# Two-tile exponentials, a row-sum column in V, and PSUM copies moved from ScalarE to VectorE in a two-layer transformer kernel

## What is computed

```python
# layer 0
x = x + attn0(layernorm(x))      # 16 heads of 128, causal, ALiBi bias
x = x + ffn0(layernorm(x))       # silu(x@gate * gs) * (x@up * us) @ down * ds, weights rounded to fp8, width 6144
# layer 1
x = x + attn1(layernorm(x))      # per token, over 32 groups of 64 channels:
                                 # qkv per group; scores[d,c,e] = q[c,d]*k[e,d]/8; softmax over e; times v; @ Wout
x = x + moe(layernorm(x))        # 8 experts of width 1408, all computed; the top one is taken, with its weight

# attn0, per head
scores = q @ k.T / sqrt(128) + slope * (kpos - qpos), -inf for kpos > qpos
out    = softmax(scores) @ v     # then all heads @ wo + bo
```

## Time and profile before

| | us |
|---|---|
| median of 2 runs | 21964.12 (21844.47 and 22083.77) |
| the profiled execution's own time | 21777.46 |
| its span on the slowest core | 21775.9 (cores: 21561.0 to 21775.9) |
| mean granted TensorE clock of the cores | 0.667 to 0.682 |
| PE busy, PEld busy | 10597.1, 4188.3 |
| DVE busy | 7421.1 |
| ACT busy | 6238.7 |
| POOL busy | 1330.9 |

### The profile page before, as it was taken

How to read it: one execution, slowest core, us unless ns; L and a number is a source line. 1 busy time by engine, 2 the same in 40 slices (tenths; PEclk the granted TensorE clock), 3 DMA queues, 4 the chain that set the end, 5 groups by cost and what they waited for, 6 DMA issues and landing times.

```text
span 21775.9 us, 138456 instructions; the slowest of 8 cores (21561.0 to 21775.9 us)
## 1 busy us (share of the span) xinstructions
PE 10597.1 (49%) x42512; PEld 4188.3 (19%) x42512; DVE 7421.1 (34%) x9984; ACT 6238.7 (29%) x5808; POOL 1330.9 (6%) x1053
## 2 busy tenths in 40 slices
PE   5855555573221432115312331002886886877876
PEld 2311112221000110002100110001332332332332
DVE  1011112100688308880387607883111111111111
ACT  3466664210222102221122202222222222222222
POOL 0000000120000000001000000000001000000000
PEclk9955556786555665557655665555786776777887
DMA  3400002794221542116412450001334344343444
GB/s 66 65 9 12 9 9 34 113 47 35 25 14 13 31 41 15 12 11 41 28 12 17 23 36 10 4 4 44 56 51 48 37 42 44 33 44 42 41 46 44
DMA packets 2403671, 711.62 MB, mean 33 GB/s; under 512 B 1986923, under 2 KB 2374268, under 8 KB 2392724
## 3 DMA queue, kind: packets, MB, share of 16 engines
q0 software_dynamic: 2203008, 484.28, 29.2%
q1 hardware_dynamic: 199958, 218.48, 3.2%
HBM read 1144.49 MB, written 209.72 MB: 62 GB/s over the span
## 4 chain that ended last, share of the span: by engine, by line
PE 36%; DVE 28%; DMA 15%; ACT 11%; issue 6%; DVEq 2%; ACTq 1%; SPq 0%; POOL 0%; POOLq 0%
DVE ctxa L953 8%; PE ps_gM L1409 6%; PE ps_uM L1415 6%; DMA out<-ostrip 6%; PE ps_dM L1486 5%; DVE zz L932 5%; DVE sct L910 5%; DMA d<-dw 5%; PE ps_sh L1172 4%; PE ps_p L326 3%; ACT L610 3%; DVE sct L948 3%; DMA u<-uw 2%; PE ps_gB L1099 2%; ACT L1496 2%
## 5 line engine op out<-in xcount | busy, mean ns | idle before, releaser
L1486 PE MATMUL ps_dM<-fuseM,dwb 128*128 128x512 bf16 x5632 | 2131.5, 555 | 31.9 <-DVEq L1440 22.7
L1099 PE MATMUL ps_gB<-xn2T,g 128*128 128x512 bf16 x3072 | 964.6, 485 | 2135.9 <-DVEq L1132 1861.7
L953 DVE TENSOR_REDUCE ctxa<-sct 128x64 bf16<-128x2048 bf16 x512 | 1831.0, 3576 | 39.5 <-issue 2.1
L920 ACT ACT_TABLE_LOAD x512 | 656.9, 1283 | 3966.7 <-DVEq L912 3966.4
L214 PE MATMUL ps_tpF<-identb,ctxa 128*128 128x128 bf16 x256 | 37.4, 301 | 3317.1 <-DVEq L957 3269.9
L1409 PE MATMUL ps_gM<-xn4T,gwb 128*128 128x512 bf16 x5632 | 1456.3, 419 | 165.6 <-DMA uwb<-muw 165.6
L1172 PE MATMUL ps_sh<-fuse,d 128*128 128x512 bf16 x3072 | 833.8, 442 | 1332.4 <-DMA d<-dw 1332.4
L1529 DVE TENSOR_SCALAR ostrip<-ps_otM,cmb 128x128 f32<-128x128 bf16 x1792 | 506.1, 344 | 2737.4 <-PE ps_otM L1506 1468.9
L1415 PE MATMUL ps_uM<-xn4T,uwb 128*128 128x512 bf16 x5632 | 1438.5, 415 | 0.0
L1496 ACT ACT_TABLE_LOAD x512 | 656.9, 1283 | 2717.9 <-PE ps_dM L1486 2717.9
L910 DVE TENSOR_TENSOR sct<-qkv 128x2048 f32<-128x2048 bf16 x512 | 1173.8, 2293 | 166.2 <-DVEq L957 137.9
(11 more groups left out here) (161 smaller groups left out, 13001.8 us busy)
## 6 DMA issues: line engine op xcount, KB each, us to landing
out<-ostrip POOLq DMA_DIRECT2D x128, 1024.0 KB, 11.1
g<-gw POOLq DMA_DIRECT2D x192, 256.0 KB, 6.9
u<-uw POOLq DMA_DIRECT2D x192, 256.0 KB, 8.7
d<-dw POOLq DMA_DIRECT2D x64, 768.0 KB, 15.1
gwb<-mgw POOLq DMA_DIRECT2D x88, 512.0 KB, 6.3
uwb<-muw POOLq DMA_DIRECT2D x88, 512.0 KB, 8.3
dwb<-mdw POOLq DMA_DIRECT2D x128, 352.0 KB, 11.8
wob<-wo POOLq DMA_DIRECT2D x64, 512.0 KB, 8.3
```

The costliest lines, as they stand in the source:

```text
L920: SS.inc(scalar.activation(out=p0[dcg % 2][:], in_=sct[dcg % 2][:], func=AF.Exp, scale=0.125))
L953: vector.tensor_reduce(out=cvw, in_=prv.transpose([0, 2, 3, 1]), axis=AX.X, op=OP.add)
L1099: tensor.matmul(ps_gB[i % 2][:], g8[i % 2][:, 128 * d:128 * (d + 1)], xn2T[tb % 2][:, 512 * d:512 * (d + 1)], start=(d == 0), stop=(d == N ...
L1486: ins = tensor.matmul(ps[:], dwb[hc % 3][:, 128 * ic:128 * (ic + 1)], fuseM[:, ic * S + 512 * tb:ic * S + 512 * (tb + 1)], start=(ic == 0) ...
```

## The change

Seven edits:

1. The QKV eviction, the copies of `krow` and `qrow`, and the evictions of the output projection, of the first FFN's down stage and of the experts' down stage go from ACT (`activation` with Copy or Identity) to DVE (`tensor_scalar` or `tensor_copy`, with `drain` and a nop for the increment). Waits and counters stay the same.
2. `ps_sT` holds two key tiles (1024 columns, two PSUM banks). PE fills both with six matmuls, ACT takes both in one Exp. There are 320 instead of 640.
3. On diagonal tiles DVE fills the columns left of the triangle with -1e30 in PSUM, ahead of Exp, instead of 0 in `PT`, and Exp runs over all 1024 columns.
4. The value matmuls also wait for the last mask (`mz_at`).
5. `vtok` has 129 columns per tile, the last of them ones, set once before the first head.
6. One matmul of 129 columns takes the place of the pair; the row sum is column 128 of `ps_av`, and `ps_r` is gone.
7. The transposed V goes to `vtok` at a step of 129 columns.

```diff
@@ qkv_pass; in the same form L514, L538 (tensor_copy), L738, L1182 (tensor_scalar with ds_sb), L1496
-                @block.scalar
-                def _(scalar, do=do, tb=tb):
-                    MM.wait(scalar)
-                    STP.wait(scalar, 4 * do + tb)
-                    EV.inc(scalar.activation(out=stgA[(4 * do + tb) % 4][:],
-                                             in_=ps_p[(4 * do + tb) % 2][:],
-                                             func=AF.Copy, scale=float(scale)))
+                @block.vector
+                def _(vector, do=do, tb=tb):
+                    MM.wait(vector)
+                    STP.wait(vector, 4 * do + tb)
+                    vector.tensor_scalar(out=stgA[(4 * do + tb) % 4][:],
+                                         in0=ps_p[(4 * do + tb) % 2][:],
+                                         scalar1=float(scale), scalar2=None,
+                                         op0=OP.mult)
+                    vector.drain()
+                    EV.inc(vector.engine_nop())
...
@@ experts, down
-                    @block.scalar
-                    def _(scalar, hc=hc, tb=tb, it=it):
-                        MM.wait(scalar)
-                        TT.wait(scalar)
-                        EV.inc(scalar.activation(out=stgm[it % 2][:],
-                                                 in_=ps_dM[it % 2][:],
-                                                 func=AF.Copy))
+                    @block.vector
+                    def _(vector, hc=hc, tb=tb, it=it):
+                        MM.wait(vector)
+                        TT.wait(vector)
+                        vector.tensor_copy(out=stgm[it % 2][:],
+                                           in_=ps_dM[it % 2][:])
+                        vector.drain()
+                        EV.inc(vector.engine_nop())
...
@@ attention tiles
-    vtok = sb3("vtok", [128, S], BF16)
+    vtok = sb3("vtok", [128, NT * 129], BF16)
...
-    ps_sT = [phA3.enter_context(nc.psum_tensor(f"ps_sT{i}", [128, 512], F32))
+    ps_sT = [phA3.enter_context(nc.psum_tensor(f"ps_sT{i}", [128, 1024], F32))
...
+        for j in range(NT):
+            vector.memset(vtok[:, 129 * j + 128:129 * j + 129], 1.0)
...
@@ scores and Exp
-            for kt in range(4 * (qtg + 1)):
+            nkt = 4 * (qtg + 1)
+            for ktp in range(nkt // 2):
+                kts = [2 * ktp, 2 * ktp + 1]
...
+                    for sub, kt in enumerate(kts):
+                        lo = 512 * sub
+                        tensor.matmul(ps[:, lo:lo + 512],
+                                      kh[h % 2][:, 128 * kt:128 * (kt + 1)],
+                                      qh[h % 2][:, 512 * qtg:512 * (qtg + 1)],
...
+                    MM.inc(ins)
...
-                        if u > 0:
-                            vector.memset(PT[:, 512 * kt:512 * kt + 128 * u], 0.0)
+                            if u > 0:
+                                vector.memset(
+                                    ps_sT[ktp % 2][:, 512 * sub:
+                                                   512 * sub + 128 * u], NEG)
...
-                    lo = 128 * u if 0 < u < 4 else 0
                     SS.inc(scalar.activation(
-                        out=PT[:, 512 * kt + lo:512 * (kt + 1)],
-                        in_=ps_sT[kt % 2][:, lo:512], func=AF.Exp))
+                        out=PT[:, 512 * kts[0]:512 * (kts[1] + 1)],
+                        in_=ps_sT[ktp % 2][:], func=AF.Exp))
...
@@ value matmuls
                     for kt in range(qt + 1):
-                        tensor.matmul(pa[:, 0:128],
-                                      PT[:, 512 * kt + 128 * u:512 * kt + 128 * (u + 1)],
-                                      vtok[:, 128 * kt:128 * (kt + 1)],
-                                      start=(kt == 0), stop=(kt == qt),
-                                      skip_group_check=True)
-                        ins = tensor.matmul(pr[:, 0:1],
-                                            PT[:, 512 * kt + 128 * u:512 * kt + 128 * (u + 1)],
-                                            onesc[:, :], start=(kt == 0),
-                                            stop=(kt == qt),
-                                            skip_group_check=True)
+                        ins = tensor.matmul(
+                            pa[:, 0:129],
+                            PT[:, 512 * kt + 128 * u:512 * kt + 128 * (u + 1)],
+                            vtok[:, 129 * kt:129 * (kt + 1)],
+                            start=(kt == 0), stop=(kt == qt))
```

More of the change, by code:

```diff
@@ L415, in build_program, with _ @@
     nh_build = 1 if probe == "att1" else NH
+    @block.vector
+    def _(vector):
+        MM.wait(vector)
+        for _i in range(4):
+            STP.c[_i].wait(vector, a2_st_at[_i])
+        for j in range(NT):
+            vector.memset(vtok[:, 129 * j + 128:129 * j + 129], 1.0)
+        vector.drain()
+        VV.inc(vector.engine_nop())
     for h in range(nh_build):
@@ L509, in _ @@
                                      start=True, stop=True))
-            @block.scalar
-            def _(scalar, j=j):
-                MM.wait(scalar)
-                SS.inc(scalar.activation(out=krow[0:1, 512 * j:512 * (j + 1)],
-                                         in_=ps_bd[:, :], func=AF.Copy))
+            @block.vector
+            def _(vector, j=j):
+                MM.wait(vector)
+                vector.tensor_copy(out=krow[0:1, 512 * j:512 * (j + 1)],
+                                   in_=ps_bd[:, :])
+                vector.drain()
+                SS.inc(vector.engine_nop())
         @block.vector
@@ L533, in _ @@
                                      start=True, stop=True))
-            @block.scalar
-            def _(scalar, j=j):
-                MM.wait(scalar)
-                SS.inc(scalar.activation(out=qrow[0:1, 512 * j:512 * (j + 1)],
-                                         in_=ps_bd[:, :], func=AF.Copy))
+            @block.vector
+            def _(vector, j=j):
+                MM.wait(vector)
+                vector.tensor_copy(out=qrow[0:1, 512 * j:512 * (j + 1)],
+                                   in_=ps_bd[:, :])
+                vector.drain()
+                SS.inc(vector.engine_nop())
         @block.vector
@@ L642, in _ @@
                     MM.wait(vector)
[L643 removed]
+                    vector.reciprocal(out=rinv[:], in_=ps_av[u % 2][:, 128:129])
                     vector.drain()
@@ L732, in build_program, with _ @@
             slab_used.append(MM.n)
-            @block.scalar
-            def _(scalar, tb=tb, do=do):
-                MM.wait(scalar)
-                TT.wait(scalar)
-                EV.inc(scalar.activation(out=stgo[it % 2][:], in_=ps_o[it % 2][:],
-                                         func=AF.Copy))
+            @block.vector
+            def _(vector, tb=tb, do=do):
+                MM.wait(vector)
+                TT.wait(vector)
+                vector.tensor_copy(out=stgo[it % 2][:], in_=ps_o[it % 2][:])
+                vector.drain()
+                EV.inc(vector.engine_nop())
             @block.tensor
@@ L1176, in _ @@
                     MM.inc(ins)
-                @block.scalar
-                def _(scalar, tb=tb, do=do):
-                    MM.wait(scalar)
-                    TT.wait(scalar)
-                    EV.inc(scalar.activation(out=stgd[do % 2][:],
-                                             in_=ps_sh[do % 2][:],
-                                             func=AF.Identity,
-                                             scale=ds_sb[:, do:do + 1]))
-                    sh_ev[do % 2].inc(scalar.nop())
+                @block.vector
+                def _(vector, tb=tb, do=do):
+                    MM.wait(vector)
+                    TT.wait(vector)
+                    vector.tensor_scalar(out=stgd[do % 2][:],
+                                         in0=ps_sh[do % 2][:],
+                                         scalar1=ds_sb[:, do:do + 1],
+                                         scalar2=None, op0=OP.mult)
+                    vector.drain()
+                    EV.inc(vector.engine_nop())
+                    sh_ev[do % 2].inc(vector.engine_nop())
                 @block.tensor
```

67 lines of the change are left out of this document (37 added, 30 removed).

## The result

| us | before | after |
|---|---|---|
| median of the runs | 21866.17 (10 runs) | 21141.49 (11 runs) |
| profiled execution, span of the slowest core | 21775.9 | 21027.3 |
| mean of the eight cores' spans | 21671 | 20802 |
| first attention, 16 heads | 2553 | 2133 |
| of a head: scores and Exp / value matmuls / the rest | 89.1 / 18.0 / 52.4 | 74.8 / 14.5 / 43.9 |

The changed kernel takes 0.9642 of the time of before, 95% interval 0.9603 to 0.9681: 3.6% less.

A forecast was written before the change was run, and what follows sets the result against it. No engine bounds the whole; ACT limited the first attention's scores, the accumulating store the expert strips. Attention 357, experts' down 205, first FFN's down 77 and output projection 25 sum to 664 us; 21964 less 664 gives 21300, range 21030 to 21550.

The forecast's parts named there:

- Scores and Exp: First attention: two tiles per Exp make PE the limit instead of ACT; 77.6 us per head, 11.5 less.
- 1.49n + 4.5: Forecast time in us of a score stage of n key tiles: 1.49 per tile on PE, plus a 4.5 us tail.
- Rival A: Score stages: PE is granted 2.4 GHz and ACT limits at 2.33 us a pair; 285 us more saved, 21015; chance 0.08.
- Value matmuls: First attention: one matmul of 129 columns instead of a pair, 0.107 us apart; 3.3 us per head saved.
- rival D: Value matmuls reading vtok at starts 258 bytes apart take 0.427 us each; 693 us back, 21993; chance 0.03.
- krow and qrow: First attention: copies on DVE cut a step from 2.69 to 1.75 us, eight times per head; 7.5 us saved.
- Experts' down: 512 evictions on DVE: blocks 2 and 3 gain, block 1 queues behind the store; 1.6 us a strip, 205 us saved.
- rival C: Expert stage gives nothing: longer wait for the store, 1.2 GHz more often; with output projection at 0, 21530; chance 0.17.
- First FFN's down: Serial chain, so all 64 evictions moved to DVE count, 1.2 us each; 77 us saved, bounds 70 and 83.
- Output projection: 64 evictions: 24 queue behind DVE's wait for stores, 40 may gain; 25 us saved, between -20 and 76.
- QKV projections: 192 evictions moved to DVE save nothing, because two PSUM tiles cover them.

The follow-up runs named there:

- exp_block: The changed kernel with the Exps of a score stage in one block of ScalarE's program instead of a block each; 21030 us, one run.
- two_score_mm: The changed kernel with the row of bounds as a 33rd row of tileA, so two matmuls a score tile instead of three; 20910 us, 0.9525.
- rows_act: The changed kernel with the krow and qrow copies back on ScalarE; 21348 us, 0.970 of before, from two executions.
- fill_act: late_act with four unread matmuls per block in the experts' down stage, where TensorE waits for ScalarE; 21367 us, 0.9715.
- late_act: The changed kernel with the evictions of the output projection and both down stages back on ScalarE; 21636 us, 0.9846.
- block1_act: The changed kernel with the eviction of token block 1 of each expert strip back on ScalarE; 20831 us, 0.9513.
- two_strips: The changed kernel with two strip buffers in the experts' down stage from the second expert on; 19929 us, 0.9136.
- col_and_late: The kernel before with only the ones column in the values and the output projection and both down stages evicted on VectorE; 21456 us, 0.9735.
- full_rows: The changed kernel with the two narrow matmuls of each score tile padded to 128 rows with zeros; 20989 us, 0.9588.

## Why the prediction was right, and where it was not

The time (21141 against 21300) and the direction were right. Of the 159 us between them 98 lie in the starting point: 21300 was reckoned from a median of two runs of before, 21964, and ten have 21866. The reduction itself was 664 us by forecast, 725 by the medians and 783 by the ratio. By its steps:

- *Scores and Exp:* 77.6 us a head forecast, 74.8 measured. TensorE as the limit is shown by table loads mattering little (exp_block) and matmuls mattering much (two_score_mm). The two short stages came as worked out (measured 10.5 and 16.6 us; 1.49n + 4.5 gives 10.5 and 16.4); the two long ones were 1.0 and 2.0 us shorter than that. Rival A was in part true: just behind the value matmuls the clock is at its upper level for some tiles, then falls. In a head's third and fourth score stage 0.19 and 0.28 of the time is at 1.00 (core 0), in the first two none, which are the two stages that came as worked out. Busy by stretch of after, the start of a fourth stage and what follows:

```profile
2205.50:2208.00 2.50, 2.50 (x12) 0.52 (x9) 0.62 (x3) 0.65 (x1) 0.00 (x0) 1.00 0.00 0
2209.00:2221.00 12.00, 10.62 (x24) 1.77 (x24) 0.00 (x0) 9.89 (x9) 0.00 (x0) 0.60 0.00 1
```

- *Value matmuls:* 3.3 us forecast, 3.4 measured, 0.107 us apart; rival D is out.
- *krow and qrow:* 7.5 forecast, 8.5 measured. The step is 1.61 us, not 1.75; the copy 0.68 as taken. rows_act confirms its engine as the cause.
- *Experts' down:* 205 us forecast, 359 measured. The hand-offs and the queueing were right in kind and within 0.2 us. The failed step was to price them at the mix of clocks of before. I had seen that the clock answers to how long PE stands, but put it on the wrong side (rival C: longer wait for the store, so lower clock). The shorter gaps between blocks did the opposite for three blocks of four, and fill_act shows that as a cause.
- *First FFN's down:* 77 forecast, 2 us lost in the profiles of before and after. The gap did shrink by 1.09 us. In the profiles of eleven kernels with this load unchanged, the time from issue to first matmul varies:

| eviction by | kernels | load to matmul, us | block, us |
|---|---|---|---|
| ScalarE | before, late_act, fill_act | 15.6, 16.3, 15.7 | 36.5, 37.3, 36.9 |
| VectorE | after, block1_act, two_strips, two_score_mm | 16.7, 15.9, 17.6, 15.9 | 36.5, 35.3, 37.5, 35.5 |
| VectorE | rows_act, col_and_late, full_rows, exp_block | 15.8, 15.7, 16.9, 16.6 | 35.5, 35.3, 36.9, 36.5 |

  Take the load out of the block, and the rest is 20.9 to 21.2 us with ScalarE and 19.4 to 20.0 with VectorE: the forecast's 1.2 us are there in every profile. The load then gives some of it back, or all, and its time was the term that the sum held fixed. With it the means of the blocks are 36.9 and 36.1, 0.8 us a block or about 50 us in all, but the blocks behind VectorE alone reach from 35.3 to 37.5. Whether the load itself is a little longer behind the faster eviction (15.9 against 16.4 in the mean), or that is chance, stays open.
- *Output projection:* 25 forecast, 0 measured; the step that failed was to leave PE's wait for wob out, which was 7.5 us and became 60.2.
- *QKV projections:* nothing forecast, nothing measured: the first head's first bound matmul starts at 1054.4 us in before and 1055.5 in after (core 0).

So mistakes of opposite sign met: 100 us too much in two stages that wait for a load, 154 too little in the stage where the clock answered, 63 too little in the attention. That the sum came as near as it did is in part luck.

## What to carry to other kernels

Before you price a shorter hand-off, ask what the engine will wait for next: here a weight load (little or nothing gained), a store (something lost) and the clock (more gained than the hand-off itself). Here a stage at half clock without gaps was cured by padding narrow matmuls with rows of zeros, one with gaps by closing them, even with work that nobody reads; either is worth only what the next limit leaves, ScalarE's 2.33 us a pair and the store. The waits for one strip buffer and for a load that was asked for too late were each worth more than the whole change, and both stood in the profile of before: DVE's 11.86 us in the earlier trace rows, POOL's 35.46 in the earlier trace rows, each behind a DMA.

## What the runs showed of the hardware that was not expected

- Three back-to-back 512-column matmuls with 128, 4 and 1 rows in use were granted 0.50 of the clock in most of a head's score stages; with 128 rows in each, 0.99 and then 0.81 (0.22 and 0.26 us apart), and 0.50 for 0.01 of the fourth stage. The rows in use count for the clock, not only whether TensorE runs. By the Trainium skill (TensorE: Matmul & The Clock Gate, "The HAM clock gate") how busy TensorE has been recently sets the clock; here a stretch busy by time but not by rows stayed at the lower level.
- Closing gaps lifts the clock: with 2.28 us between a block's matmuls and its transposes the experts' down stages are at 0.50 for 0.53 of the time, with 1.21 us for 0.37, with 2.28 us and four unused matmuls in it for 0.25.
- A table load of 1283 ns stands at the head of each block of ScalarE's program that holds an activation, also where nothing but Exp runs in between: 320 loads for 320 Exps in blocks of their own, 64 for the same 320 in 64 blocks. A wait inside the block brings none.
- The same 768 KB load by all eight cores took from 15.6 to 17.6 us in the mean of a profile with the code around it unchanged, which is more than an eviction's hand-off is worth.
